# Reordered fetches, routes and last results in a routed feed-forward and attention kernel, with other pack sizes

## The reference

```
x = x + 0.5 * ffn(layernorm(x), router_w, w1, w2)
x = x + attention(layernorm(x), Qw, Kw, Vw)          # causal, one head of 128
x = x + 0.5 * ffn(layernorm(x), router_w, w1, w2)
ffn(x):  probs = softmax(x @ router_w.T);  top 2 of 8 experts, their weights normalised to sum 1
         out = sum over the 2 experts of weight * (gelu(x @ w1[e]) @ w2[e])     # 128 -> 512 -> 128
```

## Time and profile before

| | us |
|---|---|
| median of 3 runs | 315.94 (314.13 to 319.44) |
| the profiled execution's own time | 317.9 |
| its span, first to last instruction | 315.9 |
| PE busy | 246.4 (78%) |
| POOL busy | 167.0 (53%) |
| DVE, ACT busy | 140.2, 143.4 |

### The profile page before, as it was taken

The page is one execution under the profiler, slowest core; times in us unless marked ns, Lnnn a source line. Parts: engine busy times, 40 slices in busy tenths (PEclk is TensorE's granted clock), DMA queues, the critical chain, the costliest instruction groups (busy, mean ns, idle before and its releaser), DMA issues.

```text
span 315.9 us, 6013 instructions
## 1 busy us (share of the span) xinstructions
PE 246.4 (78%) x1985; PEld 229.9 (73%) x1985; DVE 140.2 (44%) x538; ACT 143.4 (45%) x279; POOL 167.0 (53%) x196
## 2 busy tenths in 40 slices
PE   1603999999999969899498880889995999999700
PEld 0503899999999959567276560889994999999700
DVE  4589257422113334758984664454110111343305
ACT  3332765555556631446322550746554365564300
POOL 4705777374457760277171774013777775555740
PEclk9999999999999997899857797799999799999965
DMA  7980423322246751212000111411114422422115
GB/s 203 341 213 25 118 78 51 61 87 76 83 157 197 145 197 35 66 53 57 18 0 0 44 51 52 118 42 52 50 55 116 125 83 82 157 67 72 48 68 173
DMA packets 31613, 29.37 MB, mean 93 GB/s; under 512 B 3608, under 2 KB 26016, under 8 KB 31584
## 3 DMA queue, kind: packets, MB, share of 16 engines
q1 hardware_dynamic: 25552, 18.21, 19.0%
q0 software_dynamic: 4992, 10.25, 12.4%
q10 hardware_dynamic: 1040, 0.52, 0.6%
HBM read 15.69 MB, written 13.28 MB: 92 GB/s over the span
## 4 chain that ended last, share of the span: by engine, by line
PE 56%; DVE 13%; POOL 12%; DMA 9%; issue 7%; ACT 1%; POOLq 0%; SPq 0%; DVEq 0%; ACTq 0%
PE bank L1099 21%; PE bank L1111 21%; POOL slots_in L468 5%; POOL y_rows L480 3%; PE bank L1087 3%; DVE xs L896 3%; PE bank L1151 2%; POOL xb_first L457 2%; PE bank L1050 2%; PE bank L1034 2%; PE bank L1154 2%; DMA xb_pack<-slots_in 2%; DMA y_rows<-slots_out,slot_of 1%; DMA slots_in<-xn_numbered,slot_of 1%; DMA router_rows<-in_L_ffn_router_w 1%
## 5 line engine op out<-in xcount | busy, mean ns | idle before, releaser
L1099 PE MATMUL bank<-xT_pack,w_block 128*128 128x128 f32 x736 | 100.5, 282 | 5.7 <-DVE xT_pack L850 5.7
L1111 PE MATMUL bank<-w_sb,act 128*128 x736 | 98.1, 279 | 0.2 <-issue 0.2
L1099 PEld LDWEIGHTS bank<-xT_pack,w_block 128*128 128x128 f32 x736 | 92.4, 198 | 6.6 <-DVE xT_pack L850 6.6
L1111 PEld LDWEIGHTS bank<-w_sb,act 128*128 128x128 f32 x736 | 90.5, 195 | 0.8 <-issue 0.7
L566 ACT ACTIVATE act<-bank 128x512 f32<-128x512 f32 x92 | 54.9, 597 | 77.9 <-PE bank L1099 77.8
L560 ACT COPY w_block<-w_sb 128x512 f32 x92 | 56.0, 613 | 16.6 <-issue 8.9
L457 POOL DMA_INDIRECT xb_first<-xn_rows,row_in x46 | 44.8, 974 | 34.2 <-DVE row_in L819 15.9
L480 POOL DMA_INDIRECT y_rows<-slots_out,slot_of x32 | 30.4, 951 | 26.8 <-DMA slots_out<-yb_pack 17.7
L468 POOL DMA_INDIRECT slots_in<-xn_numbered,slot_of x32 | 30.8, 961 | 16.9 <-issue 8.8
L850 DVE COPY xT_pack<-bank 128x512 f32<-128x512 f32 (+2 forms) x28 | 16.6, 594 | 51.2 <-PE bank L1087 51.1
L494 POOL DMA_INDIRECT final_rows<-xb_first,row_of x23 | 22.0, 958 | 28.7 <-DVE xb_first L869 22.3
(11 more groups left out here) (123 smaller groups left out, 253.6 us busy)
## 6 DMA issues: line engine op xcount, KB each, us to landing
w_sb<-in_L_ffn_w SPq DMA_DIRECT2D x8, 512.0 KB, 7.8
xb_pack<-slots_in SPq DMA_DIRECT2D x10, 258.0 KB, 2.9
slots_out<-yb_pack SPq DMA_DIRECT2D x10, 256.0 KB, 2.7
slots_in<-numbered SPq DMA_DIRECT2D x6, 387.0 KB, 4.8
y_rows<-final_rows SPq DMA_DIRECT2D x8, 256.0 KB, 4.1
xs<-in_L_attn_x SPq DMA_DIRECT2D x4, 256.0 KB, 4.0
out<-xs SPq DMA_DIRECT2D x8, 128.0 KB, 1.8
xb_first<-xn_rows,row_in POOLq DMA_INDIRECT x46, 2.9
```

Source lines behind the costliest of these rows:

```text
L1099: mm = nc.tensor.matmul(h_of(c)[:, q * P:(q + 1) * P], w1_block[c % WIDE_BUFS][:, q * P:(q + 1) * P], xT_pack[n % 2][:, j * P:(j + 1) * P] ...
L1111: mm = nc.tensor.matmul(y_ps[n % 2][:, j * D:(j + 1) * D], act[c % WIDE_BUFS][:, q * P:(q + 1) * P], w2_sb[:, bass.ds(at + q * D, D)], sta ...
```

## The change

- Pack sizes become 1, 2, 2, 2, eight of 4, 3, 2, 1, 1: 16 packs where there were 14. For the results of the last phase there is a list of its own, `Y_PACK_SIZES`, in which the last eleven blocks go as 2, 2 and seven single ones; PE, DVE, ACT and POOL count results by it.
- All fetches of the first phase stand ahead of the gathers. A fetch of group 1 waits only until the buffer's former block is turned; from the fifth pack on each waits for the pack four before it to have landed, and some packs for a product count (`FETCH_WAITS`).
- `ranks(2)` stands between queries and values on PE, five instead of three pieces of route 2 before the copies of the values on DVE, and the two pieces of `gates(2)` go beside attention's first two units instead of the last phase's blocks. In the last phase logits come at s = 3 (4), ranks at 5 (7), DVE's pieces by `LAST_PIECES`.
- No result is returned before the last scatter; returns wait for the products in `RETURN_WAITS`. Each group's returned rows have a table and a semaphore of their own, and group 1's results lie in the buffer `numbered`, free by then, so they wait for no reuse.

The diff, without the hunks that only declare or rename tables, row numbers and semaphores:

```diff
@@ -40,12 +40,17 @@
 PACK = 4
-PACK_SIZES = [1, 2] + [PACK] * 10 + [2, 1]
-assert sum(PACK_SIZES[:7]) == MAX_BLOCKS and sum(PACK_SIZES) == BLOCKS
+PACK_SIZES = [1, 2, 2, 2] + [PACK] * 8 + [3, 2, 1, 1]
+assert sum(PACK_SIZES[:8]) == MAX_BLOCKS and sum(PACK_SIZES) == BLOCKS
 PACKS = len(PACK_SIZES)
 LAST_PACKS = 2 * PACKS - GROUP_PACKS
+Y_PACK_SIZES = PACK_SIZES + PACK_SIZES[:11] + [2, 2] + [1] * 7
+assert sum(Y_PACK_SIZES) == 2 * BLOCKS
+Y_PACK_STARTS = [sum(Y_PACK_SIZES[:n]) for n in range(len(Y_PACK_SIZES))]
 H_BANKS = 4
...
@@ -136,7 +141,7 @@
         xb_first = sb("xb_first", [P, MAX_BLOCKS, D])
-        y_third = xb_first
+        y_last = [xb_first, numbered[:, :, 0:D]]
         row_of = sb("row_of", [P, BLOCKS], I32)
...
@@ -242,8 +246,9 @@
         TRANSPOSES_BESIDE = 1
-        LOGITS_BESIDE = 4
-        RANKS_BESIDE = 7
+        LOGITS_BESIDE = 3
+        RANKS_BESIDE = 5
+        LAST_PIECES = {0: 1, 3: 1, 4: 2, 5: 1, 6: 1, 7: 1}
         SECOND_COPIES_BESIDE = 3, 5
...
@@ -256,14 +261,13 @@
         RSTD_OF_ROWS = {0: 1, 2: 4}
-        FIRST_RETURN = 11
-        FIRST_RETURN_WAITS = (29, 33, 37, 41)
-        FETCHED_AMID = ((11,), (12, 13), (), ())
-        LAST_SCATTER_WAITS = {3: 12, 6: 15}
-        RETURNED_AHEAD = 2
-        RETURN_WAITS = {2: 18, 3: 20, 4: 22, 5: 25}
-        THIRD_LOADED_BEFORE = 2 * PACKS - 1
-        LAST_COMBINES = (37, 39, 41, 43)
+        FETCH_WAITS = {4: 1, 5: 3, 6: 6, 7: 8, 9: 15, 10: 18, 11: 20, 12: 23, 13: 25}
+        FIRST_RETURN_WAITS = (31, 34, 36)
+        LAST_SCATTER_WAITS = {3: 10, 6: 14}
+        RETURNED_AHEAD = 0
+        RETURN_WAITS = {0: 17, 2: 19, 4: 21, 5: 24, 6: 26}
+        THIRD_LOADED_BEFORE = 2 * PACKS - 3
+        LAST_COMBINES = (38, 40, 42, 44)
...
@@ -273,6 +277,14 @@
             return max(n for n in range(2 * PACKS) if PACK_STARTS[n] <= c)
+        def y_pack_of(c):
+            return max(n for n in range(len(Y_PACK_SIZES)) if Y_PACK_STARTS[n] <= c)
+        def ends_y_pack(c):
+            n = y_pack_of(c)
+            return c + 1 == Y_PACK_STARTS[n] + Y_PACK_SIZES[n]
...
@@ -377,7 +389,7 @@
                 if n == THIRD_LOADED_BEFORE:
-                    sp.wait_ge(third_returned, 16 * MAX_BLOCKS)
+                    sp.wait_ge(returned[0], 16 * MAX_BLOCKS)
                     load_final(0)
...
@@ -388,8 +400,7 @@
                 store_out(t)
-            for n in range(2 * PACKS - PACK_BUFS, 2 * PACKS):
-                sp.wait_ge(final_stored[n % PACK_BUFS], 16 * transfers_until(n, LAST_PACKS, PACK_BUFS))
+            sp.wait_ge(returned[1], 16 * MAX_BLOCKS)
             load_final(1)
...
@@ -450,8 +461,12 @@
                     pool.wait_ge(rows_known, g + 1)
-                if n > 2:
-                    pool.wait_ge(xT_ready, n - 1)
+                if g:
+                    pool.wait_ge(xT_ready, pack_of(blocks_of(n)[-1] - MAX_BLOCKS) + 1)
+                if n >= FETCH_SEMS:
+                    pool.wait_ge(x_fetched[n % FETCH_SEMS], 16 * transfers_until(n - FETCH_SEMS, 0, FETCH_SEMS))
+                if n in FETCH_WAITS:
+                    pool.wait_ge(h_ready, FETCH_WAITS[n])
                 for c in blocks_of(n):
...
@@ -485,29 +500,27 @@
-                pool.wait_ge(row_known, n - PACKS + 1)
+                c = Y_PACK_STARTS[n]
+                pool.wait_ge(row_known, pack_of(c) - PACKS + 1)
                 pool.wait_ge(y_copied, n + 1)
-                for j, c in enumerate(blocks_of(n)):
-                    b = c - BLOCKS
-                    rows, stored = ((y_third[:, b, :], third_returned) if n < LAST_PACKS else
-                                    (yb_pack[n % PACK_BUFS][:, j, :], final_stored[n % PACK_BUFS]))
+                for b in range(c - BLOCKS, c - BLOCKS + Y_PACK_SIZES[n]):
+                    g = b // MAX_BLOCKS
                     pool.indirect_dma_start(
-                        final_rows, bass.IndirectOffsetOnAxis(ap=row_of[:, b:b + 1], axis=0),
-                        rows, None).then_inc(stored, 16)
+                        final_rows[g], bass.IndirectOffsetOnAxis(ap=row_of[:, b:b + 1], axis=0),
+                        y_last[g][:, b % MAX_BLOCKS, :], None).then_inc(returned[g], 16)
             normalise_rows(0)
-            for n in range(FIRST_RETURN):
+            for n in range(PACKS):
                 gather_in(n)
             for i in range(GT // 2):
-                pool.wait_ge(h_ready, FIRST_RETURN_WAITS[i])
+                if i:
+                    pool.wait_ge(h_ready, FIRST_RETURN_WAITS[i - 1])
                 some_of(returning, TOP * GT // 4)
-                for n in FETCHED_AMID[i]:
-                    gather_in(n)
             for _ in chain(returning, gather(1)):
...
@@ -519,7 +532,7 @@
             scatter(3)
-            for n in range(PACKS + RETURNED_AHEAD, 2 * PACKS):
+            for n in range(PACKS + RETURNED_AHEAD, len(Y_PACK_SIZES)):
                 if n - PACKS in RETURN_WAITS:
...
@@ -562,7 +575,7 @@
                     if c >= WIDE_BUFS:
-                        sc.wait_ge(y_ready, pack_of(c - WIDE_BUFS) + 1)
+                        sc.wait_ge(y_ready, y_pack_of(c - WIDE_BUFS) + 1)
                     nc.scalar.activation(act[c % WIDE_BUFS][:], h_of(c)[:], ACT.Gelu).then_inc(act_ready, 1)
...
@@ -853,33 +866,32 @@
                 def copy_y(n):
-                    size = len(blocks_of(n))
-                    here = yb_pack[n % PACK_BUFS][:, 0:size, :]
+                    size = Y_PACK_SIZES[n]
                     dve.wait_ge(y_ready, n + 1)
-                    if n >= LAST_PACKS + PACK_BUFS:
-                        dve.wait_ge(final_stored[n % PACK_BUFS],
-                                    16 * transfers_until(n - PACK_BUFS, LAST_PACKS, PACK_BUFS))
-                    elif n >= LAST_PACKS:
-                        dve.wait_ge(y_stored[n % PACK_BUFS], 16 * packs_until(n - PACKS // PACK_BUFS * PACK_BUFS, 0))
-                    elif n >= PACKS:
-                        b = PACK_STARTS[n] - BLOCKS
-                        here = y_third[:, b:b + size, :]
-                    elif n >= PACK_BUFS:
-                        dve.wait_ge(y_stored[n % PACK_BUFS], 16 * packs_until(n - PACK_BUFS, 0))
-                    v.tensor_copy(here.rearrange("p j d -> p (j d)"),
-                                  y_ps[n % 2][:, 0:size * D]).then_inc(y_copied, 1)
+                    if m:
+                        b = Y_PACK_STARTS[n] - BLOCKS
+                        here = y_last[b // MAX_BLOCKS][:, b % MAX_BLOCKS:b % MAX_BLOCKS + size, :]
+                    else:
+                        here = yb_pack[n % PACK_BUFS][:, 0:size, :]
+                        if n >= PACK_BUFS:
+                            dve.wait_ge(y_stored[n % PACK_BUFS], 16 * packs_until(n - PACK_BUFS, 0))
+                    v.tensor_copy(here, y_ps[n % 2][:, 0:size * D].rearrange("p (j d) -> p j d", d=D)
+                                  ).then_inc(y_copied, 1)
                 for n, turn_at in first_product_at(m):
-                    for j, c in enumerate(blocks_of(n)):
-                        beside(c - first + 2)
+                    behind = blocks_of(n - 1) if n > m * PACKS else ()
+                    for j in range(max(len(blocks_of(n)), len(behind))):
+                        if j < len(blocks_of(n)):
+                            beside(PACK_STARTS[n] + j - first + 2)
                         if j == turn_at and n + 1 < (m + 1) * PACKS:
                             copy_xT(n + 1)
-                    if n > m * PACKS:
-                        copy_y(n - 1)
-                copy_y((m + 1) * PACKS - 1)
+                        if j < len(behind) and ends_y_pack(behind[j]):
+                            copy_y(y_pack_of(behind[j]))
+                for c in blocks_of((m + 1) * PACKS - 1):
+                    copy_y(y_pack_of(c))
...
@@ -990,19 +1002,20 @@
             pieces = route(2)
-            for _ in range(3):
+            for _ in range(5):
                 next(pieces)
             rest(pieces)
-            attend(1, lambda u: None)
-            pieces = chain(rstd_of(GT, GT), normalise(NORM_OF_ROUTE[3]), gates(2), iter([None]), route(3))
+            pieces = gates(2)
+            attend(1, lambda u: next(pieces, None))
+            pieces = chain(rstd_of(GT, GT), normalise(NORM_OF_ROUTE[3]), route(3))
             for _ in range(4):
             def beside_last(s):
-                if s < MAX_BLOCKS:
-                    next(pieces, None)
+                for _ in range(LAST_PIECES.get(s, 0)):
+                    next(pieces)
                 if s in LAST_COMBINES:
...
@@ -1103,16 +1116,17 @@
                     c = PACK_STARTS[n] + j
-                    at = offset(c)
+                    at, y = offset(c), y_pack_of(c)
+                    k = c - Y_PACK_STARTS[y]
                     pe.wait_ge(act_ready, c + 1)
-                    if j == 0 and n >= 2:
-                        pe.wait_ge(y_copied, n - 1)
+                    if k == 0 and y >= 2:
```

(17 more changed lines are left out.)

5 lines of the change are left out of this document (2 added, 3 removed).

## The result

The changed kernel took 303.01 us (median of 4 runs, 302.31 to 305.14), the kernel before beside it 317.37 (314.13 to 319.44): ratio 0.9592, 95% interval 0.9485 to 0.9698. The profiled execution took 303.0 with a span of 301.2; before it was 317.9 and 315.9. So 14.7 us went between the two traces, where 12.4 were forecast. In later runs the unedited changed kernel took 302.92 on a second chip (before: 320.85; 0.9464, 0.9398 to 0.9530) and 305.37 on a third (before: 317.44; 0.9573, 0.9525 to 0.9620).

What follows compares the result with a forecast made beforehand. Pauses in TensorE's chain and POOL's late returns were taken to bound the kernel. Terms 5.1 + 2.6 + 6.7 - 2.0 = 12.4 us took the profiled 317.9 to 305.5, a median of 303.6; range 300.0 to 310.

Steps and rivals of the forecast that it cites:

- What bounds the kernel: Expert phases are a closed chain of TensorE work; only shortening its four pauses, the last being POOL's late returns, gains time.
- Part 1: First phase: fetches ahead of all gathers remove PE's pause near 118 us and the half-rate work behind it, 5.1 us.
- rival (b): First phase: the combine still waits because gathers start no sooner; 5.1 us missing, 308.7 us; 12%.
- Part 2: Attention: ranks ahead of the value products bring the scatter and the last phase's start 2.6 us sooner.
- Rival (d): Attention: ranks before the values give nothing since another wait ends last; 306.2 us; 6%.
- Part 3: Last phase's opening: pauses of 2.9 and 1.0 us; 2.0 us lost, plus 2.0 for a slower clock.
- the fall of the clock: Last phase's opening: PE drops to half rate after the 2.9 us pause, charged 2.0 us.
- rival (a): Last phase's opening: no fall of the clock; gain 14.4 us, so 301.6 us; 25%.
- Part 4: Last scatter starts sooner, so PE's pause before group 1's rows goes with a margin of 1.7; 6.0 us return.
- Part 5: End: last return issued 3.7 us behind the last product's start, not 6.5; 6.7 us in all, packs' own share 2.7.
- The sum: Whole kernel: 5.1 + 2.6 + 6.7 - 2.0 = 12.4 us saved, so a median of 303.6 us.

Runs made afterwards that it cites:

- The lone edit: Kernel before with all fetches of the first phase ahead of the gathers, pack sizes left: 312.73 us beside 320.85, ratio 0.9701.
- the two repetitions: Changed kernel run again without any edit, on a second and a third chip: 302.92 us and 305.37 us.
- the first repetition: Changed kernel run again without any edit on the second chip: 302.92 us.
- the delayed scatter: Changed kernel with the results of blocks 0 to 4 returned ahead of the last scatter: 309.81 us beside 305.37.
- The late route: Changed kernel with the last phase's logits and ranks at blocks 4 and 7 again, one piece a block: 301.26 us.
- the copy ahead: Changed kernel with the copy of xT ahead of the two pick pieces at s = 4 in the last phase: 300.39 us.

## Why the prediction was right, step by step

- **What bounds the kernel**: right. Only the pauses of PE's chain and POOL's issues behind it moved the time; the last phase gets shorter only when a pause or a return goes.
- **Part 1**: right, 4.85 for 5.1. The gathers start at 88.65 and end at 107.50 (forecast 89.4 and 109.4, the latter the end of the last). The lone edit showed that the order of the fetches does it, 5.2 behind its opening: rival (b) is out.
- **Part 2**: right in kind, 3.0 for 2.6, shown by undoing it. I had taken 0.4 for hand-overs that the trace doesn't have. Rival (d) is out.
- **Part 3**: the pauses were right to 0.3 us (2.86 and 0.69 for 2.9 and 1.0), the fall of the clock came, and rival (a) with it is out. Mis-sized: the opening cost 4.7 and not 4.0 (4.2 and 4.5 in the two repetitions). Two errors go against each other. The fall was charged too high, 2.0 for the 1.5 to 1.8 up to block 5. And block 3's product came 12.64 us behind the phase's start, where the forecast has 209.5 - 197.75 = 11.75. Of this most is that the product at 190.77 took 1.91, its counterpart in the earlier trace rows at 202.16 took 1.16. That is chance between executions and no doing of the change: in the first repetition it took 1.16, and block 3's came at 11.92.
- **Part 4**: the 6.0 us came (5.9), and the rows were there in time: last scatter 227.18, plus the 5.3 us that the delayed scatter shows from 233.42 to 238.70, is 232.5, against 234.12 asked. Margin 1.6, forecast 1.7. But the reason that I gave holds only in part. I put the gain down to the sooner route and the returns' order together. Counted from the phase's start, the scatter began at 19.8, for 22.5 before, and all of that is the order, since the slots came no sooner (18.9 for 18.7). Held for product 10, it ended only 0.9 sooner, 40.5 for 41.4, where I had 1.8. What also closed the pause is that PE asked for the rows later, at 47.4 for 42.9, by the opening that part 3 spoils; the two parts together gave 1.2, where I had 2.0. With the old opening the rows, there at 45.8, would still have come about 2.9 late (an estimate from these numbers). The late route shows the order nearly enough by itself, 0.64 of pause left, though PE asks for the rows 3.2 sooner there (at 44.2) than in the changed kernel. Whether a sooner route with three results ahead would have been enough isn't shown. Only with the copy ahead does the sooner route tell: the last scatter is issued 36.7 behind the phase's start, where it was 40.5, and 39.3 with the late route. A late route with the copy ahead wasn't tried.
- **Part 5**: 3.76 behind the start of the last product for 3.7. Of the 2.8 the singles are 1.5 to 1.9, shown. POOL's return at 263.42 took 1.12 and that at 266.11 took 1.11, each beside a combine, where their neighbours take 0.96. That agrees with the Trainium skill (GPSIMD Engine Reference, Specifications) on vector instructions with two SBUF inputs, at 0.15 us each. It isn't so for every one: the returns at 270.90 and 275.94 also overlap a combine in part and took 0.96.
- **The sum**: 12.4 for 14.7 between the traces. Without the two items that no run shows to be the change's doing, 1.3 at the start and 1.9 at the queries, it is 11.5: my terms were 0.9 too high in all, and chance brought the difference of these two executions above them. That the median came within 0.6 us of the forecast is partly due to that. Against the kernel before on the same chip the differences of medians were 14.4, 17.9 and 12.1; of the 17.9, part 1 alone gave 8.1, and undoing part 2 gave 3.0.

## What to carry to other kernels

Where one engine issues all indirect transfers, look for what stands in its order ahead of the transfer that the bottleneck waits for next: the fetches ahead of the gathers were worth 5 us here, five results ahead of the scatter cost 5.5, and no work was removed or added. When a pause is gone, look whether the data came sooner or the bottleneck later; here it was more the second. Work put forward on the engine that also copies for the bottleneck is paid for at the next copy; put the copy first, and the work behind it. Judge such a step by the distance between two events of its own stage, since a kernel's time carries 1 to 3 us from other stages. Even that distance carries chance: the spread was 0.4 us over three traces of the changed kernel, and 2.5 over the two that have the last phase of before.

## What the hardware did that I had not expected

- The same work behind the same idle time ran at either rate, as it did behind the pause of 1.43 in the last phase (full rate before, half rate with the fetches first). The four query products took 3.44 us at a granted clock of 0.57 before, and 1.96 at 1.00 after, both behind 1.33 us of idle. Of the twelve later profiles eleven had 1.96 or 1.97; the one with the copy of xT ahead, whose edit lies far behind this place, had 3.24 at 0.61. In windows (stretch, length, PE busy, granted clock, DMA share, GB/s) of the kernel before, from 132 us:

```profile
132.00:136.00 4.00, 4.00 (x10) 0.57 0.15 45
```

and in the changed kernel, from 124 us (all engines in this one):

```profile
124.00:128.00 4.00, 3.74 (x13) 1.91 (x14) 3.62 (x17) 1.76 (x3) 1.93 (x2) 1.00 0.12 33
```

- The unedited kernel's upper heap of times (305.3 to 305.6) has one profile, and it differs from the first in phase one's opening: a product behind 0.58 us of idle took 2.08, in the first 1.16 behind 0.59; one that starts at 45.80 there starts at 48.35, 0.67 of it from a later start. The granted clock reads 1.00 in both from 28 to 40 us, so a row's duration is the better witness there. The profiles of two edited kernels, fetches first and ranks late, have such a product too (2.08 and 2.07). Timeline of PE in the repetition:

```profile
33.70 2.08 PE L1112 MATMUL bank<-xT_pack,w_block 128*128 128x128 f32 x8 [0.58 <-DVE xT_pack L863]
...
37.27 1.32 PE L1112 MATMUL bank<-xT_pack,w_block 128*128 128x128 f32 x8
```

and of the changed kernel's first profile:

```profile
32.88 1.16 PE L1112 MATMUL bank<-xT_pack,w_block 128*128 128x128 f32 x8 [0.59 <-DVE xT_pack L863]
```

- The router table lands at 6.3 us in the trace of before and at 4.7 to 5.9 in the thirteen others. Of the 1.56 us between before and after 1.28 are left at phase one's first transposes. What sets it isn't shown.
